# Another order of the steps in the mLSTM part of a decoder layer, on all five engines

## The reference, cut to what matters

```python
x = x + attn(layernorm(x), W_qkv, W_out)             # 16 heads of 16, causal softmax
x = x + mlstm(layernorm(x), ctx, ctx, ifgate_w, ...) # 8 heads of 32
x = x + moe(layernorm(x), router_w, ...)             # 8 experts, best 2, exact gelu

# mlstm, per sequence and head
pre   = 15 * tanh((concat(q, k, v) @ ifgate_w.T + ifgate_b) / 15)
lf    = cumsum(log_sigmoid(f_pre))
log_d = lf[t] - lf[s] + i_pre[s]  where t >= s, else -inf
d_mat = exp(log_d - max_s(log_d))
s_mat = (q @ k.T / sqrt(32)) * d_mat
h     = s_mat @ v / (max(|sum_s s_mat|, exp(-max)) + 5e-5)
h     = h * rsqrt(mean(h * h) + 1e-6) * (1 + outnorm_w)
```

## Time and profile before

| | |
|---|---|
| median of 3 runs | 968.09 us (965.02 to 971.19) |
| profiled execution, its own time | 962.93 us |
| its span, first to last instruction | 961.2 us |
| mean granted clock of TensorE | 0.967 of full speed |
| busy: PE, DVE, ACT, POOL | 92%, 61%, 51%, 52% |
| shares of the chain that ended last | PE 80%, DVE 7%, ACT 5%, issue 3% |

### The profile page before, as it was taken

How to read it: one execution, slowest core, us unless ns; L and a number is a source line. 1 busy time by engine, 2 the same in 40 slices (tenths; PEclk the granted TensorE clock), 3 DMA queues, 4 the chain that set the end, 5 groups by cost and what they waited for, 6 DMA issues and landing times.

```text
span 961.2 us, 31757 instructions
## 1 busy us (share of the span) xinstructions
PE 887.1 (92%) x11966; PEld 653.0 (68%) x11966; DVE 586.2 (61%) x1292; ACT 487.4 (51%) x839; POOL 496.3 (52%) x705
## 2 busy tenths in 40 slices
PE   5999999999997689899998988999999999999995
PEld 3667667667665356565564776778888888878783
DVE  4856766766764456777777657455555555555552
ACT  3667677677666367566455542333333333333331
POOL 2556666566565333366666667534444434444432
PEclk9999999999999799999888899999999999999998
DMA  9222443443445654455453233433332333233322
GB/s 283 70 57 67 93 129 90 96 127 90 92 119 121 172 183 132 146 177 179 144 162 118 90 86 89 87 62 51 48 51 47 53 49 52 46 52 52 47 34 23
DMA packets 133197, 92.96 MB, mean 97 GB/s; under 512 B 75712, under 2 KB 114112, under 8 KB 132928
## 3 DMA queue, kind: packets, MB, share of 16 engines
q1 hardware_dynamic: 119760, 73.10, 28.2%
q0 software_dynamic: 13296, 17.83, 11.1%
HBM read 54.65 MB, written 37.32 MB: 96 GB/s over the span
## 4 chain that ended last, share of the span: by engine, by line
PE 80%; DVE 7%; ACT 5%; issue 3%; DMA 2%; SPq 2%; another core or an unknown queue 1%; POOL 0%; DVEq 0%; ACTq 0%; POOLq 0%
PE pair L933 19%; PE pair L949 12%; PE pair L951 6%; PE pair L634 5%; PE pair L671 5%; PE pair L657 4%; PE pair L811 3%; PE pair L607 3%; PE pair L684 2%; PE pair L825 2%; PE pair L829 2%; PE pair L861 2%; PE pair L900 2%; PE pair L786 1%; PE pair L837 1%
## 5 line engine op out<-in xcount | busy, mean ns | idle before, releaser
L933 PE MATMUL pair<-XTs,WU 128*128 128x128 bf16 x3408 | 283.9, 219 | 5.9 <-DVE XTs L1269 2.9
L933 PEld LDWEIGHTS pair<-XTs,WU 128*128 x3408 | 238.1, 98 | 71.7 <-issue 8.7
L1603 POOL DMA_INDIRECT out_d<-XB x71 | 116.1, 1635 | 207.4 <-DVE XB L1291 174.0
L949 PE MATMUL pair<-WD,Hh 128*128 x568 | 214.8, 379 | 1.3 <-issue 1.3
L1469 ACT ACTIVATE Hf<-pair 128x512 f32<-128x512 f32 x142 | 84.8, 597 | 219.5 <-PE pair L933 207.9
L1282 DVE CAST Hh<-Hf 128x512 bf16<-128x512 f32 x142 | 64.5, 454 | 172.1 <-ACT Hf L1469 166.9
L951 PE MATMUL pair<-WD,Hl 128*128 x568 | 154.7, 272 | 0.0
L1284 DVE TENSOR_TENSOR Hl<-Hf,Hh 128x512 bf16<-128x512 f32 x142 | 99.5, 701 | 4.9
L1514 POOL TENSOR_SCALAR_AFFINE_SELECT PT<-PT 128x512 f32<-128x512 f32 (+1 forms) x96 | 73.9, 787 | 44.2 <-ACT PT L1320 28.7
L1576 POOL DMA_INDIRECT xs_scr<-XB,WGf x64 | 66.9, 1045 | 31.7 <-issue 18.2
L1488 POOL TENSOR_TENSOR LS<-LS,mhalf 128x2 f32<-128x2 f32 x48 | 34.1, 711 | 94.6 <-DVE LS L976 93.9
(11 more groups left out here) (243 smaller groups left out, 1728.9 us busy)
## 6 DMA issues: line engine op xcount, KB each, us to landing
XB<-xs_scr SPq DMA_DIRECT2D x71, 130.0 KB
STG<-wup_in SPq DMA_DIRECT2D x32, 256.0 KB
q_scr<-SPL SPq DMA_DIRECT2D x16, 512.0 KB, 4.2
STG<-wdn_in SPq DMA_DIRECT2D x32, 256.0 KB
o_scr<-On SPq DMA_DIRECT2D x32, 128.0 KB, 4.2
Mm<-o_scr SPq DMA_DIRECT2D x16, 256.0 KB, 3.0
CnT<-ctxt_in SPq DMA_DIRECT2D x16, 256.0 KB, 4.0
CX<-ctx_in SPq DMA_DIRECT2D x16, 256.0 KB, 4.4
```

What stands on the lines that cost most here:

```text
L933: t = e.matmul(upb(j, k)[:, 128 * (fm % 4):128 * (fm % 4) + 128], WU[:, bass.ds(reg[j] * 4096 + off, 128)], XTs[:, r, hx, dk, :], start=n ...
L949: e.matmul(yb[r][:, 0:512], Hh[:, r, hsl], WD[:, bass.ds(reg[i] * 4096 + 512 * fk, 512)], start=fk == 0, stop=False, skip_group_check=True)
L1603: e.indirect_dma_start(out=out, out_offset=bass.IndirectOffsetOnAxis(ap=XS[:, i % NX, 256:257].bitcast(I32), axis=0), in_=Yf[:, i % NY, :] ...
```

## The change

The five strings of `ORDER` are permuted. Every word stays, with its lag and unit, so every instruction and every DMA of the program stays; the appended tail stays too, apart from the steps that the rounds have already done, which are the same.

```diff
 ORDER = {
-    "tensor": "D:0:0 B6:4 R4:5 PV:1:1 S:0:0 rest:0:0 D:0:1 PV:1:2 rest:0:1 D:0:2 B5:3 S:0:1 PV:0:0 rest:0:2 B4:1 S:0:2",
-    "vector": "B4x:2 rest:0:0 S:0:0 R5:5 R6:5 rest:0:1 B5s:2 S:0:1 rest:0:2 R2:4 B4:1 first:14 R3:4 S:0:2 R1:3",
-    "scalar": "rest:0:2 split:0 B4p:2 D:0:0 B5n:3 split:0 rest:0:0 D:0:1 rest:0:1 split:0 R1:4 B3:1 B5:3 D:0:2",
-    "gpsimd": "B4p:2 rest:0:0 sc:0 R6:5 split:0 split:0 sc:0 rest:0:1 sc:0 split:0 rest:0:2 B5s:2",
-    "sync": "load:0 rest:0:2 B1:0:1 B1:-1:0 rest:0:0 B4o:2 rest:0:1 row:15",
+    "tensor": "D:0:0 B6:4 PV:1:1 R4:5 S:0:0 rest:0:0 rest:0:1 D:0:1 PV:1:2 B5:3 D:0:2 S:0:1 PV:0:0 rest:0:2 B4:1 S:0:2",
+    "vector": "B4x:2 R5:5 R6:5 rest:0:0 S:0:0 rest:0:1 B5s:2 S:0:1 first:14 R2:4 B4:1 R3:4 rest:0:2 S:0:2 R1:3",
+    "scalar": "split:0 B4p:2 D:0:0 rest:0:0 R1:4 rest:0:2 split:0 B5n:3 D:0:1 rest:0:1 B3:1 D:0:2 split:0 B5:3",
+    "gpsimd": "sc:0 split:0 rest:0:0 B4p:2 rest:0:1 sc:0 R6:5 sc:0 rest:0:2 split:0 B5s:2 split:0",
+    "sync": "load:0 B1:-1:0 rest:0:0 rest:0:2 B1:0:1 B4o:2 rest:0:1 row:15",
 }
```

## The result

The new order is slower. It runs in 985.8 us (982.0 to 989.0, four runs); beside it the kernel before took 969.6. The ratio is 1.0176 with a 95% interval of 1.0136 to 1.0217, that is 17 us more (13 to 21). The forecast was 981, between 958 and 994. The profiled execution has a span of 984.1 us and a mean clock of 0.953, against 961.2 and 0.967.

The account below looks back on a forecast made before the run. PE was taken to bound the mLSTM stage, with no slack in the experts behind it. Terms 12.5 - 3.9 + 5.0 - 2.1 - 0.7 + 1 + 1 = +12.8 us, on the runs' median 968.1, gave 981, range 958 to 994.

Parts of the forecast that it names:

- The four scatters: In five odd rounds POOL's run delays PE's signals, so B3 and PV unit 0 wait: +12.5 us; old waits credited 3.9.
- The clock left at zero: PE's lower clock: up to 14 us of loss already there; stalls might move such stretches, so no change counted.
- The steady rounds otherwise: Other edits of the steady rounds on DVE, PE and SP: -2.1, -0.7, +1 and +1 us.
- The leftover steps: Leftover attention steps in rounds 1 to 5, reordered on the engines, make PE wait more: +5.0 us, between 2 and 8.
- `first`: DVE does this step ahead of B4 of round 14, in idle time, removing a PE wait: -2.1 us.
- B5 ahead of D unit 2: On PE in the steady rounds, this order hides the wait for ACT: -0.7 us.
- R5 and R6: Placed ahead of the first score product, they delay it by some 1.3 us in even rounds: +1 us in all.
- The context: SP issues its DMA behind the next round's decays and queries; mostly hidden from PV unit 0: +1 us, 0 to 8.
- One sign of being wrong: Odd rounds as long as the even ones would speak against the forecast; no size given.
- the scatters hold nothing: Rival: scatters cost nothing at their new place and nearly nothing else changes: +0.3 us, 968; chance 0.20.
- Faster: Rival: the run misses the end of PV unit 2, old waits and some low-clock time go: 958 us; chance 0.20.
- The context was late: Rival: the context lands late as a rule, costing PV unit 0 some 0.7 us in 13 rounds: 990 us; chance 0.12.

Follow-up runs that it names:

- faster mix: Kernel before, but from round 6 new PE and ACT orders, new DVE with `first` old, and POOL's B5s between the run's two pairs; ratio 0.9843.
- fastest mix: The faster mix with one POOL split moved ahead of each round's first pair of scatters; ratio 0.9833 to the kernel before.

## Why the prediction was right

The time and the place of the loss were right; two thirds of the loss in rounds 6 to 14 came by a term that was left at zero. By its own steps:

- **The four scatters** (+12.5, credit 3.9). Right as a mechanism: in rounds 7 and 11 signals are held to 0.7 and 0.9 us after the run, B3 starts late, PV unit 0 waits for it, and the waits at B4 go. Three sizes were off. The hold is longer: B3 started at 9.5 and 10.6 us into rounds 7 and 11, not at 7.7 to 9, since the run began at 3.6 and 4.9. It came in two odd rounds, not in five: in the others PE was at the lower clock for part of the round (mean 0.74 to 0.77) and ended PV unit 2 behind the run. And pairs in rounds 6, 8 and 12 cost 0.7, 1.4 and 1.2 more. PE's waits for B3 are 8.8 us in all, below 12.5; undone, POOL's order is worth 18, above the 8.6 of the sum. The rest is put down to the clock.
- **The clock left at zero** is the term that was missing. PE's busy time of rounds 6 to 14 grew by 10.5 us. The held round is followed by one at the lower level: round 8 took 17.2 us, round 12 16.7, against 11.05 for rounds 10 and 14 of the same trace. In the five kernels that lost 1.3% or more and kept the run of four, the clock of rounds 6 to 14 is 0.81 to 0.84; before it was 0.93, with the run broken 0.94, with POOL's old order 1.00. That the wait brings the low clock is argued from the order in time, each fall after a wait for B3; no run here separates the two, and a wait does not always bring it: in the faster mix the clock stays at 1.00 from 422.5 to 510 us, across three waits of 1.4 us for score products.
- **"The steady rounds otherwise" and the addition of terms.** I added the scatters to the other edits as if each had its price. The new POOL order alone costs 0.2%, the other four orders alone nothing (0.9991), and together they cost 1.8%: the edits set where in PE's round the run lies. The forecast said from what point the hold decides, but not that the old orders put the run behind it: it placed the run at 1.9 us, or a little later, from rows of the old orders, and there POOL's new line starts it at 4.9 to 6.0.
- **The leftover steps** (+5.0, between 2 and 8): 3.9. GA waits 1.42 us where 1.5 stood, the context 0.66 (0.4), B5 behind GT 2.22 (2.5), the score behind Gs 0.66 (0.9), B4 behind GE 1.09 (1.2). D unit 2 of round 1 waits 1.12 instead of 2.15, a gain of 1.0 where I took 0.4.
- **`first`** (-2.1) failed. The wait of 2.7 at a score became one of 3.15 at B6, so the balance is +0.4. I had named B6 and given it 0.6.
- **B5 ahead of D unit 2** (-0.7): the wait for ACT fell from 0.7 to 0.2. **R5 and R6** (+1): waits for score products from round 6 to 14 are 0.5 us; the pair that they bring forward cost by B3. **The context** (+1): no wait in the steady rounds; its one wait, 0.66, is that of round 2 above.
- **Small slips of the sums.** PE's waits from 385 to 545 us add up to 11.2 us, not 10.5: three short waits for B3 (0.7) were left out. The upper end of 994 adds the 8 us of the context to a sum that already holds 1 of them.

So the sum of +12.8 was near the measured 17 because a missing clock term and an overrated count of held rounds offset each other in part; that it came so near is luck. One sign of being wrong came in part too: the even rounds 8 and 12 are as long as the odd ones, by the wait for B3 behind a pair and the low clock.

Of the rivals, "the scatters hold nothing" is out. The Trainium skill's page "SBUF — State Buffer", section "Who interferes with whom", says that DMA never contends with a compute engine and that TensorE and ScalarE wait on nobody. Here, in round 7, ACT's B3 started 4.2 us after the end of PE's work beside a run of scatters, PE waited 2.08 us for it, and a loss of 1.6% went with one split between the scatters; the measurement decides. "Faster" failed on its own condition, since in rounds 7 and 11 the run did contain the end of PV unit 2. The context was late once.

## What to carry to other kernels

- Before moving a burst of GpSimd's indirect DMAs, write down which signal of PE falls in it and who waits for that signal. Break bursts with other POOL work; the place in PE's round counts, not the engine's own list.
- Edits of several engines' orders need not add up: here neither POOL's line alone nor the other four alone cost anything that can be told. Test one engine's line undone and the same line alone.
- Where PE bounds the stage, compare its busy time for the same matmuls, not only its waits. A wait may cost twice, itself and a slower clock behind it, as the order in time suggests here.

## What the runs showed of the hardware

While POOL issues scatters, signals of PE reach ACT and DVE late, and PE itself pauses between matmuls (0.34 us in round 7 of the kernel after). In the kernel after, the signal of PV unit 2 was 4.2 and 4.9 us late in rounds 7 and 11, until 0.7 and 0.9 us after the run of four. How long the hold lasts depends on where in the run the signal falls: 1.1 and 1.7 us where it fell 0.2 to 0.3 us behind the start of a run (round 9 with POOL's new order alone, round 11 with its run earlier), and in three rounds (7 and 13 with SP old, 11 with `first` old) B3 started 0.5 us before the last scatter ended. Why it differs, and by what path the signals are held, isn't shown: no run replaced the scatters by other DMAs.

A DVE operation with two inputs in SBUF is stretched by POOL's split. In the faster mix the second operation of B4x takes 2.86 us beside two splits in a row:

```profile
442.71 2.86 DVE L1169 TENSOR_TENSOR XB<-XB,hh 128x512 f32<-128x512 f32 x1
442.74 2.27 POOL L1559 TENSOR_TENSOR WD<-STG,WD 128x512 bf16<-128x512 f32 x2
```

In the fastest mix, with a scatter there and the split after it, it takes 0.74:

```profile
434.44 0.74 DVE L1169 TENSOR_TENSOR XB<-XB,hh 128x512 f32<-128x512 f32 x1
434.46 0.98 POOL L1583 DMA_INDIRECT xs_scr<-XB,WGf  x1 [0.30 <-issue]
435.46 1.17 POOL L1559 TENSOR_TENSOR WD<-STG,WD 128x512 bf16<-128x512 f32 x1
```

The same section of the Trainium skill says that a DVE instruction with two SBUF inputs contends with a GpSimd instruction that reads SBUF; by that rule, the traces agree.
